# Column and row stage of a Hartley-transform convolution on other TensorE tiles, with stores of four equal parts per image

## The reference

```
x_ht = dht_2d(x)
out_ht = out_ht.at[:, :, :M1, :M2].set(compl_mul2d(x_ht[:, :, :M1, :M2], w1))
y = dht_2d(out_ht) / (H * W)
y = gaussian_smoothing_4d(y)
return y * mask
```

## Time and profile before

| what | value |
|---|---|
| median of three runs | 155.11 us (154.5 to 155.58) |
| profiled execution, its own time | 156.23 us |
| span in its trace | 154.3 us |
| granted clock of PE, mean | 0.976 |
| PE busy | 132.8 us (86%) |
| DVE, ACT, POOL busy | 62.0, 36.4, 39.4 us |
| read from and written to memory | 20.19 MB, 16.78 MB |
| stores | 8 of 768 KB, 16 of 640 KB |

### The profile page before, as it was taken

One profiled execution on the slowest core, in us unless ns is written; L12 is line 12 of the kernel. 1 busy time (PEld: TensorE's weight loads), 2 busy tenths in 40 slices (PEclk: granted clock), 3 DMA queues, 4 the chain that ended last, 5 costly groups with the idle time before them and its releaser, 6 DMA issues.

```text
span 154.3 us, 5759 instructions
## 1 busy us (share of the span) xinstructions
PE 132.8 (86%) x2574; PEld 80.7 (52%) x2574; DVE 62.0 (40%) x127; ACT 36.4 (24%) x85; POOL 39.4 (26%) x21
## 2 busy tenths in 40 slices
PE   6967468999999799999797699999999999999600
PEld 5523222545454445455565688677585775755200
DVE  1033850464646354546139312243434433344400
ACT  3000410111111011111218412433333333332300
POOL 8999000314645180917520000000000000000000
PEclk9999996999999999999999999999999999999995
DMA  4999999999999996000000000069999999999997
GB/s 113 351 359 269 370 351 348 363 378 362 382 350 362 350 350 207 0 4 4 0 4 2 4 4 0 6 206 330 314 340 302 340 309 325 337 314 338 345 340 237
DMA packets 34438, 37.31 MB, mean 242 GB/s; under 512 B 800, under 2 KB 33824, under 8 KB 34416
## 3 DMA queue, kind: packets, MB, share of 16 engines
q1 hardware_dynamic: 34272, 36.90, 72.8%
q10 hardware_dynamic: 144, 0.07, 0.4%
HBM read 20.19 MB, written 16.78 MB: 240 GB/s over the span
## 4 chain that ended last, share of the span: by engine, by line
PE 73%; DMA 8%; SPq 6%; ACT 3%; issue 2%; DVE 1%; DVEq 0%
PE ps L559 19%; PE ps L373 15%; DMA x_ring<-x 8%; PE ps L538 8%; PE ps L517 6%; PE ps L390 6%; PE ps L361 3%; PE ps L495 3%; ACT mixin L615 3%; PE ps L426 3%; PE ps L413 3%; PE ps L445 2%; SPq L315 2%; SPq L322 2%; SPq L325 2%
## 5 line engine op out<-in xcount | busy, mean ns | idle before, releaser
L373 PE MATMUL ps<-x_ring,k_wide 64*64 64x512 f32 x256 | 32.6, 626 | 6.0 <-DMA x_ring<-x 6.0
L718 DVE STREAM_TRANSPOSE y_sb<-ps 128x1024 f32<-128x1024 f32 x16 | 20.0, 1250 | 33.0 <-PE ps L373 33.0
L559 PE MATMUL ps<-cols,k_wide 128*64 128x330 f32 (+1 forms) x192 | 30.2, 464 | 0.0
L559 PEld LDWEIGHTS ps<-cols,k_wide 128*64 128x64 f32 x192 | 13.2, 136 | 12.7 <-issue 4.7
L373 PEld LDWEIGHTS ps<-x_ring,k_wide 64*64 64x64 f32 x256 | 8.5, 137 | 20.6 <-issue 12.9
L590 DVE COPY rows<-ps 128x330 f32<-128x330 f32 (+1 forms) x24 | 12.6, 525 | 13.3 <-PE ps L559 12.7
L871 POOL TENSOR_TENSOR spread<-parts,k_wide 128x960 f32<-128x960 f32 (+2 forms) x6 | 10.1, 1688 | 23.6 <-ACT parts L642 23.6
L361 PE MATMUL ps<-idle 128*128 128x256 f32 x46 | 14.3, 463 | 1.2 <-DVE idle L709 1.2
L590 ACT COPY rows<-ps 128x330 f32<-128x330 f32 (+1 forms) x24 | 11.1, 462 | 17.7 <-PE ps L559 16.6
L390 PE MATMUL ps<-y_sb,k_wide 64*64 64x96 f32 x512 | 14.2, 248 | 0.0
L538 PEld LDWEIGHTS ps<-k_wide,modes 64*64 64x64 f32 x384 | 11.8, 134 | 3.9 <-issue 3.9
(11 more groups left out here) (60 smaller groups left out, 98.5 us busy)
## 6 DMA issues: line engine op xcount, KB each, us to landing
x_ring<-x SPq DMA_DIRECT2D x16, 1024.0 KB, 11.4
out<-rows SPq DMA_DIRECT2D x16, 640.0 KB, 4.9
out<-rows SPq DMA_DIRECT2D x8, 768.0 KB, 6.4
w_sb<-mix_w SPq DMA_DIRECT2D x2, 960.0 KB, 12.2
k_wide<-wide SPq DMA_DIRECT2D x1, 528.0 KB, 12.5
k_tab<-narrow SPq DMA_DIRECT2D x1, 361.2 KB, 10.5
k_wide<-wide SPq DMA_DIRECT2D x1, 321.0 KB, 12.0
k_wide<-wide SPq DMA_DIRECT2D x1, 128.0 KB, 5.6
```

The lines of the kernel that those rows point to most:

```text
L373: last = nc.tensor.matmul(ps[64 * t:64 * t + 64, 2 * g + e, :], k_wide[rows_in, O_LT + 64 * r:O_LT + 64 * r + 64], x_ring[rows_in, u, 8 * ...
L559: last = nc.tensor.matmul(ps[64 * g:64 * g + 64, B_F[k % 3], 0:nt * NW], const(O_LH + s * H + r * H // 2, (1, H // 2)), cols[:, u, 6 * g:6 ...
L718: nc.vector.transpose(view(y_sb[:, g, 0, 0, 0:1], (1, 1024)), view(ps[:, 2 * g, 0:1], (1, 1024))).then_inc(y_out, 1)
```

## The change

The column stage no longer packs three channels in one stationary operand. It takes one channel at a time: 32 places of `modes` on 64 partitions, a 64x32 tile of PE. Four quads per image (even or odd channels, half c of them), each with 4x2 channels and two partition halves, 16 matmuls, go alternately to banks 3 and 4; ACT copies quads 0 and 2, DVE quads 1 and 3. The result has a channel's cosines in 32 partitions and its sines in 32 beside them, two channels above each other (x = 0 and 1, eight channel pairs apart). The row stage then contracts over 64 partitions: in each of 4 steps (half c, row parity r) four matmuls of 264 columns run on the four 64x64 tiles of PE, into banks 0 and 5 (r = 0) or 6 and 7 (r = 1). ACT copies what came from the lower 64 partitions, DVE the rest. The row table has H = 128 columns in place of 384. Per image there are four stores, of 4 pairs of channels each, and each waits for one of the two engines only.

```diff
-    lh = np.zeros((3, 128, H))
-    for s in range(3):
-        for a in range(MODES + 1):
-            lh[s, s * NF + a] = rows @ np.cos(th * h * a)
-            lh[s, 64 + s * NF + a] = rows @ np.sin(th * h * a)
+    lh = np.zeros((2, 2, BPAD, H))
+    for a in range(NF):
+        lh[:, 0, a] = rows @ np.cos(th * h * a)
+        lh[:, 1, a] = rows @ np.sin(th * h * a)
 
     wide = np.zeros((128, NC128), np.float32)
...
-        B_T, B_F = 3, (5, 6, 7)
+        B_T, B_F = 3, ((0, 5), (6, 7))
...
-        CHUNKS = [(s, r, 6 if s == 0 else 5) for s in range(3) for r in range(2)]
-        PLACED = (1, 1, 2, 2, 3, 3)
-        ROUND = 3
...
             def store(n, u):
-                for s in range(3):
-                    sp.wait_ge(rows_act, n * ROUND + PLACED[2 * s])
-                    sp.wait_ge(rows_dve, n * ROUND + PLACED[2 * s])
-                    pairs = to_pair[bass.ds(n, 1), :, s:HC:3, :].rearrange("a q k e -> q (a k) e")
-                    sp.dma_start(pairs, rows[:, u, s:HC:3, :, :].rearrange("q k r w -> q k (r w)")
-                                 ).then_inc(out_done[u], 16)
+                for c in range(2):
+                    for x, half_rows in enumerate((rows_act, rows_dve)):
+                        sp.wait_ge(half_rows, n * 4 + 2 * c + 2)
+                        first = 8 * x + PAIRS * c
+                        pairs = to_pair[bass.ds(n, 1), :, first:first + PAIRS, :].rearrange("a q k e -> q (a k) e")
+                        sp.dma_start(pairs, rows[:, u, first:first + PAIRS, :, :].rearrange("q k r w -> q k (r w)")
+                                     ).then_inc(out_done[u], 16)
 
             for n in range(2):
                 store(n, n)
...
+            def to_columns(n, u):
 
                 pe.wait_ge(modes_act, n + 1)
                 pe.wait_ge(modes_dve, n + 1)
-                if from_(n, 1):
-                    pe.wait_ge(cols_act, n)
-                    pe.wait_ge(cols_dve, n)
-
-            def to_columns(n, u):
-
-
-                for t in range(TRIPLES):
-                    first = t // 6 * HC + t % 6 * 3
-                    for half in (slice(0, 64), slice(64, 128)):
-                        last = nc.tensor.matmul(ps[half, B_T + t // 6, (t % 6) * NW:(t % 6 + 1) * NW],
-                                                modes[half, u, first * NF:first * NF + 64],
-                                                k_wide[half, O_TW:O_TW + NW], start=True, stop=True)
-                    if t in (5, TRIPLES - 1):
-                        last.then_inc(t_done, 1)
-
-            def to_rows(n, u, part, next_columns=False):
-
-                if part == 0:
-                    pe.wait_ge(cols_act, n + 1)
-                    pe.wait_ge(cols_dve, n + 1)
-                for k in range(3 * part, 3 * part + 3):
-                    s, r, nt = CHUNKS[k]
-
-                    if k >= 3:
-                        pe.wait_ge(rows_dve if k % 2 == 0 else rows_act, n * ROUND + PLACED[k - 3])
-                    elif from_(n, 1):
-                        pe.wait_ge(rows_dve if k % 2 == 0 else rows_act, (n - 1) * ROUND + PLACED[k + 3])
-                    if k == 2 and next_columns:
-                        await_modes(n + 1)
-                    for g in range(2):
-                        last = nc.tensor.matmul(ps[64 * g:64 * g + 64, B_F[k % 3], 0:nt * NW],
-                                                const(O_LH + s * H + r * H // 2, (1, H // 2)),
-                                                cols[:, u, 6 * g:6 * g + nt, :], start=True, stop=True)
+                for quad in range(QUADS):
+                    copied = cols_act if quad % 2 == 0 else cols_dve
+                    if 2 * n + quad // 2 > 0:
+                        pe.wait_ge(copied, 2 * n + quad // 2)
+                    for i in range(PAIRS):
+                        for x in range(2):
+                            at = (quad // 2 * HC + quad % 2 * PAIRS + i + 8 * x) * NF
+                            for p in range(2):
+                                to = BPAD * (2 * x + p)
+                                last = nc.tensor.matmul(ps[to:to + BPAD, B_T + quad % 2, i * NW:(i + 1) * NW],
+                                                        modes[64 * p:64 * p + 64, u, at:at + BPAD],
+                                                        k_wide[64 * p:64 * p + 64, O_TW:O_TW + NW],
+                                                        start=True, stop=True)
+                    last.then_inc(t_done, 1)
+
+            def to_rows(n, u, c):
+
+                pe.wait_ge(cols_act if c == 0 else cols_dve, 2 * n + 2)
+                for r in range(2):
+                    step = 4 * n + 2 * c + r
+                    if step >= 2:
+                        pe.wait_ge(rows_act, step - 1)
+                        pe.wait_ge(rows_dve, step - 1)
+                    for x in range(2):
+                        for e in range(2):
+                            quad = 2 * e + c
+                            last = nc.tensor.matmul(ps[64 * e:64 * e + 64, B_F[r][x], 0:PAIRS * NW],
+                                                    k_wide[64 * x:64 * x + 64, O_LH + 64 * r:O_LH + 64 * r + 64],
+                                                    cols[64 * x:64 * x + 64, u, quad * PAIRS:(quad + 1) * PAIRS, :],
+                                                    start=True, stop=True)
                     last.then_inc(f_done, 1)
 
...
-        def place_rows(copy, k, u):
-
-            s, r, nt = CHUNKS[k]
-            return copy(view(rows[:, u, s, r, 0:1], (3 * 2 * H, nt), (H - HALF, 2), (1, HALF)),
-                        view(ps[:, B_F[k % 3], 0:1], (NW, nt), (HALF, 2), (1, HALF)))
+        def place_rows(copy, step, x, u):
+
+            c, r = step // 2, step % 2
+            return copy(view(rows[:, u, 8 * x + PAIRS * c, r, 0:1], (2 * H, PAIRS), (H - HALF, 2), (1, HALF)),
+                        view(ps[:, B_F[r][x], 0:1], (NW, PAIRS), (HALF, 2), (1, HALF)))
 
         def unmix(copy, bank):
...
                 act.wait_ge(turned, n + 1)
                 if from_(n, 2):
-                    act.wait_ge(t_done, n * 2 - 2)
+                    act.wait_ge(t_done, n * QUADS - QUADS)
                 place_modes(nc.scalar.copy, 0, u).then_inc(modes_act, 1)
 
             def cols_step(n, u):
-                act.wait_ge(t_done, n * 2 + 1)
-                nc.scalar.copy(cols[:, u, 0:6, :], ps[:, B_T, 0:6 * NW]).then_inc(cols_act, 1)
-
-            def rows_step(n, u, it, chunks):
-                if from_(it, 1) and chunks[0] < 3:
-                    act.wait_ge(out_done[u], it * 48)
-                for k in chunks:
-                    act.wait_ge(f_done, n * 6 + k + 1)
-                    place_rows(nc.scalar.copy, k, u).then_inc(
-                        rows_act, 1)
+                for quad in (0, 2):
+                    act.wait_ge(t_done, n * QUADS + quad + 1)
+                    nc.scalar.copy(cols[:, u, quad * PAIRS:(quad + 1) * PAIRS, :],
+                       ps[:, B_T + 0, 0:PAIRS * NW]).then_inc(cols_act, 1)
+
+            def rows_step(n, u, it, c):
+                if from_(it, 1) and c == 0:
+                    act.wait_ge(out_done[u], it * 64)
+                for step in (2 * c, 2 * c + 1):
+                    act.wait_ge(f_done, n * 4 + step + 1)
+                    place_rows(nc.scalar.copy, step, 0, u).then_inc(rows_act, 1)
 
             def write_step(n, u, it):
-                rows_step(n, u, it, (0, 2))
+                rows_step(n, u, it, 0)
                 cols_step(n + 1, 1 - u)
                 modes_step(n + 2, u)
-                rows_step(n, u, it, (4,))
+                rows_step(n, u, it, 1)
 
             modes_step(0, 0)
...
-            def rows_step(n, u, it, chunks):
-                if from_(it, 1) and chunks[0] < 3:
-                    dve.wait_ge(out_done[u], it * 48)
-                for k in chunks:
-                    dve.wait_ge(f_done, n * 6 + k + 1)
-                    place_rows(nc.vector.tensor_copy, k, u).then_inc(
-                        rows_dve, 1)
+                for quad in (1, 3):
+                    dve.wait_ge(t_done, n * QUADS + quad + 1)
+                    nc.vector.tensor_copy(cols[:, u, quad * PAIRS:(quad + 1) * PAIRS, :],
+                       ps[:, B_T + 1, 0:PAIRS * NW]).then_inc(cols_dve, 1)
+
+            def rows_step(n, u, it, c):
+                if from_(it, 1) and c == 0:
+                    dve.wait_ge(out_done[u], it * 64)
+                for step in (2 * c, 2 * c + 1):
+                    dve.wait_ge(f_done, n * 4 + step + 1)
+                    place_rows(nc.vector.tensor_copy, step, 1, u).then_inc(rows_dve, 1)
 
             def write_step(n, u, it):
```

More of the change, by code:

```diff
@@ L17 @@
 NF = MODES + 1
-TRIPLES = 12
+QUADS = 4
+PAIRS = 4
 BPAD = 32
@@ L43 @@
 O_LH = O_TW + NW
-O_TURN = O_LH + 3 * H
+O_TURN = O_LH + H
 NC128 = O_TURN + S * Q * C
@@ L206, in constants @@
     wide[:, O_TW:O_LH] = tw
```

(41 more changed lines are left out.)

1 line of the change is left out of this document (removed).

## The result

The changed kernel took 173.63 us (median of four), the kernel before 155.35; the ratio is 1.117 with a 95% interval of 1.109 to 1.125. The profiled execution took 173.81 us, its span is 171.1. Forecast were 153.3 us and a range that ended at 158. It was wrong, in sign too. Some executions here are longer at a lower granted clock; they are left out of the ratios, and where too few are left for a ratio (e3's first series, e4, e5, e8), the remaining times stand by themselves.

A forecast was written before the change was run, and what follows sets the result against it. PE and DMA run almost level; with PE's period cut from 6.50 to 5.99 us, DMA's 6.12 binds. Stores end at 151.2 instead of 153.1: gain 1.85 us, forecast 153.3 us, range 151.8 to 158.0.

The forecast's parts named there:

- the sum's new period: PE's time per image in the row stage: column transform 2.40, turning 1.25, row steps 2.34, together 5.99 us.
- so DMA binds by 0.7 us: End of the stores: DMA finishes its last bytes at 151.2 us, PE's own bound is 150.5.
- Rival A: Column transform bound by weight loads and issue, 25.6 ns a record, 3.30 us; time 159.7 us; chance 0.22 from 21.7 ns on.
- The 25 ns between matmuls: Column transform: a skill's rule on least spacing of matmul starts would make it 3.2 us; kept as a rival view.
- Rival B: PE's column transform or wait chains: losses cancel the row transform's gain, period 6.31, time 155.1 us; chance 0.28 with neighbours.
- Rival C: Stores: they flow faster, at 362 GB/s, so PE sets the end, time 152.0 us; chance 0.05.
- Rival D: PE's clock: the small new waits, 0.3 us, lower the granted clock; chance 0.01.
- Four row steps: Row transform: four steps in a row, 0.50 us each plus 0.84 us until a bank is free, 2.34 us.
- the waits on copies: New PE waits for PSUM banks to be copied out, about 0.3 us twice per image.
- The sums 2.34 and 2.40: PE's row steps and column transform with their waits: 3x0.50+0.84 = 2.34 and 3x0.52+0.84 = 2.40 us.
- Stores of 0.5 MB: Output: 32 stores of 0.52 MB replace 24 larger ones at the same 343 GB/s, counted as zero cost.
- One side sum: Bound for the stores: at 362 GB/s, the loads' rate, they would take 2.7 us less.

The follow-up runs named there:

- e3: Kernel before, each row matmul cut into pieces of two triples (184 records per image in all, same result); 157.96 us, the one time that could be compared.
- e4: Changed kernel with two stores of 1 MB per image in place of four of 0.5 MB; 181.19 us.
- e5: Changed kernel with the column stage as 16 full 128x128 matmuls, 128 records per image, stores taking every second pair; 161.83 and 162.56 us.
- e8: Kernel before with row matmuls cut into pieces and turning matmuls of 96 or 64 columns halved, 240 records per image; 172.24 and 173.40 us against 154.51.
- e7b: Changed kernel with half as many column matmuls and turning in two matmuls (128 records per image, wrong output), repeated with five rounds; ratio to before 0.995.
- e2: Changed kernel storing a quarter of the bytes, PE's program untouched; 156.17 us.
- e9: Changed kernel storing a thirty-second of the bytes, PE's program untouched; 156.87 us.
- e3b: The kernel of e3 run once more; 159.29 us, ratio to before 1.021 (1.010 to 1.033).

## Why the prediction was wrong, step by step

**The step that failed** is the sum's new period, "2.40+1.25+2.34 = 5.99 us", and with it "so DMA binds by 0.7 us". It took PE's supply of instructions as free. From 112.31 to 150.31 us a block of 256 instructions came every 5.4 us, and so an image's 224 records took 9.6 us where 5.99 were forecast. PE's row stage lasts from 94.07 to 161.3, 67.3 us, against 48.1 in e7b: 19.2 more, of which the gaps are 14.8 and the half clock about 3.5.

**The trace of before had two signs of it.** Its page has the instruction queue with 20 packets and 0.33 MB, and in the load phase, with the DMA engines full of loads, its chain has this piece between two groups of one run of matmuls:

```profile
51.27 0.20 PE ps L455 x6
51.47 1.13 issue
52.60 0.39 PE ps L455 x2
```

That is a gap of the same kind: a packet of the program ended at 51.09, 1.5 us before PE went on. In its row stage 136 records in 6.5 us ask for a block every 6.1 us, slower than they came in e8 (4.75) and in the changed kernel (5.4).

**Rival A had the right sign and the wrong cause.** It priced a column transform of 3.3 us by issue and weight loads; it takes 2.27 in e2 and 2.47 here, and 2.40 was forecast. The 25 ns between matmuls that the prediction cites from the Trainium skill, "TensorE: Matmul & The Clock Gate", section "Wait — 56ns, not 53.3ns?", would give 3.2. The traces do not agree: the 128 records in 2.27 us are 17.7 ns apart, and in e8 the turning's 120 records in 1.48 us are 12.3 ns apart. So the row L451 was the better guide, and the weighing of the two was right while both missed the limit that decided. **Rival B**, margin too thin, could not be tried in this kernel; in e7b the period of 5.91 us stayed under the DMA's 6.12. **Rival C** found nothing: full windows show 339 to 341 GB/s. **Rival D** I gave 0.01, because the waits that I knew were 0.3 us; after two of the gaps of 2 to 3 us the clock did fall.

**The other steps held, two of them by luck.** Four row steps 2.37 (forecast 2.34); copies 0.43 and 0.39; turning 1.25; and the waits on copies are there, but smaller: 0.20 us once per image among the row steps (forecast 0.34), and in the column transform none of PE (forecast 0.33). The sums 2.34 and 2.40 came near by luck, since the work itself was longer, 2.17 and 2.27 us in place of 2.00 and 2.07. Stores of 0.5 MB flow as the larger ones, 339 GB/s in full windows and 341 in e7b; the first are issued at 100.29 where 99.4 would follow from the start at 94.07 without the first gap. One side sum was off: stores at 362 GB/s would save 2.6 us, not 2.7. The forecast also carried over the kernel before's 1.9 us outside the span, where this kernel has 2.3 to 3.0.

The Trainium skill, "Runtime: NRT & Kernel Launch", section "Instruction fetch mechanics", describes blocks of 16 KiB, 256 instructions, which each sequencer fetches by its own DMA queue. The packets and the 126 to 128 records between gaps agree. It calls the cost of a block boundary mostly hidden; here one cost up to 2.65 us, and the measurement decides.

None of the kernels tried beats the one before and gives its output. By an estimate from the 5.4 us per block, a form with at most some 145 records per image (128/5.4x6.12) would be needed; the two runs with 128 records won 1.2% and 0.5%, with intervals that reach to nothing.

## What to carry to other kernels

Count PE's instructions per stage, weight loads included, and divide by 256: in these runs a block came every 4.1 us with nearly idle DMA engines (e9) and every 4.75 to 5.4 us under full stores (e8 and the changed kernel). That is about 25 float32 matmul records per microsecond (128 in 4.75 to 5.4 us); a long stage that asked for more starved, whether its tiles were the new or the old ones. Fewer, longer matmuls can be worth more than fuller use of the array. In a trace look for "issue" gaps inside a run of equal matmuls, for the same number of instructions between them, and for a 16 KB packet of the instruction queue that ends 1.2 to 1.6 us before each gap does. A wait put down to a copy that had ended before the wait began can be such a gap too.

## What the runs showed of the hardware

- There is little reserve: e3 ran 28 us at one block per 4.5 us before its first gap. In e3b the packets came every 5.2 us meanwhile (98.57 to 119.50, four intervals), and a packet started only after PE had entered the block before it.
- Where weight loads of 128 columns set the pace, a float32 record took 116 ns (e5). Records with loads of 64 columns came every 32 ns (48 in 1.55 us) and, on four tiles, with loads of 32 columns every 17.7 ns (e2). The Trainium skill, "TensorE: Matmul & The Clock Gate", section "LDWEIGHTS (loading the stationary operand)", gives columns divided by 1.2 in ns, so 107 for 128 columns: e5 measured 8% more. No run here has loads of 64 or 32 columns one after another on a single tile as the limit, so the rule is not tried for them.
- After a gap of 2.65 us the granted clock was 0.50 for the next 6 us, and after one of 2.50 us it fell too (0.72 from 130 to 136 us). The length of the gap does not settle it: after 2.00 and 2.64 us in the same run it stayed at 1.00, and in e2 it fell after 1.68 us (0.57 from 124 to 128 us) but not after 1.57. In e9, with gaps up to 1.24 us, it was 1.00 from 95 to 151 us.
